# Causal mask of the score maxima: from TensorE products to a VectorE add-and-maximum

## The reference

```python
scores = jnp.einsum('bhqd,bhkd->bhqk', Q, K) / scale
causal = jnp.tril(jnp.ones((s, s), dtype=bool))
scores = jnp.where(causal, scores, jnp.float32(-100000.0))
A = jax.nn.softmax(scores, axis=-1)
```

## Time and profile before

| | |
|---|---|
| median of three runs | 945.94 us (940.37 to 948.93) |
| the profiled execution | 943.07 us, span 941.3 us |
| mean granted TensorE clock | 0.889 of full speed |
| TensorE busy | 694.3 us, 74% |
| VectorE busy | 472.5 us, 50% |
| ScalarE busy | 359.9 us, 38% |
| GpSimd busy | 332.1 us, 35% |

### The profile page before, as it was taken

One profiled execution on the slowest core, in us unless ns is written; L12 is line 12 of the kernel. 1 busy time (PEld: TensorE's weight loads), 2 busy tenths in 40 slices (PEclk: granted clock), 3 DMA queues, 4 the chain that ended last, 5 costly groups with the idle time before them and its releaser, 6 DMA issues.

```text
span 941.3 us, 14542 instructions
## 1 busy us (share of the span) xinstructions
PE 694.3 (74%) x4531; PEld 480.2 (51%) x4531; DVE 472.5 (50%) x1013; ACT 359.9 (38%) x912; POOL 332.1 (35%) x324
## 2 busy tenths in 40 slices
PE   0441222374678888987899888999859999999993
PEld 0441111142233343533345442788749999989983
DVE  6435556597676776485777874445411122111210
ACT  0122333244358654456364557411203222322220
POOL 1113454485688852301141116301612211111222
PEclk9856555596599999999999999899999999999997
DMA  6999788689674302998911003676979999999971
GB/s 214 303 264 304 274 283 306 227 285 331 202 228 155 113 2 101 276 330 267 373 61 46 1 2 122 237 253 218 305 233 303 331 311 327 311 339 378 348 199 22
DMA packets 136207, 216.15 MB, mean 230 GB/s; under 512 B 10357, under 2 KB 102058, under 8 KB 135978
## 3 DMA queue, kind: packets, MB, share of 16 engines
q1 hardware_dynamic: 114808, 150.78, 48.4%
q0 software_dynamic: 16784, 61.51, 21.3%
q10 hardware_dynamic: 4546, 3.08, 1.1%
HBM read 160.87 MB, written 56.37 MB: 231 GB/s over the span
## 4 chain that ended last, share of the span: by engine, by line
DMA 33%; PE 29%; DVE 18%; issue 9%; POOL 6%; ACT 2%; SPq 1%; POOLq 1%; DVEq 0%; ACTq 0%
DMA results<-arena,home 13%; DVE arena L1752 8%; DMA result<-arena,home 7%; PE psum L1455 6%; PE psum L1281 5%; DMA arena<-table,tap_col 4%; PE psum L1469 3%; PE psum L1517 3%; POOL pairs_x L1034 3%; DMA arena<-padded,band_col 3%; DMA arena<-qk_rows 3%; PE psum L1526 2%; PE psum L1415 2%; PE psum L1294 1%; PE psum L1322 1%
## 5 line engine op out<-in xcount | busy, mean ns | idle before, releaser
L1201 ACT ACTIVATE arena<-psum 128x512 f32<-128x512 f32 (+3 forms) x384 | 170.2, 491 | 131.1 <-PE psum L1469 99.0
L1752 DVE TENSOR_REDUCE arena<-psum 128x2 f32<-128x1024 f32 (+2 forms) x192 | 176.0, 954 | 61.6 <-PE psum L1287 47.0
L1251 ACT ACTIVATE arena<-psum,b_cols 128x128 f32<-128x128 f32 x312 | 84.7, 382 | 232.4 <-PE psum L1517 229.1
L1526 PE MATMUL psum<-arena 128*128 128x256 f32 x624 | 144.6, 386 | 11.5 <-DVE arena L2084 11.5
L1517 PE MATMUL psum<-arena 128*128 128x128 f32 x1248 | 148.2, 278 | 6.5 <-issue 3.6
L1517 PEld LDWEIGHTS psum<-arena 128*128 128x128 f32 x1248 | 146.9, 194 | 9.7 <-issue 8.1
L1281 PE MATMUL psum<-arena 96*128 96x512 bf16 (+3 forms) x384 | 107.5, 347 | 34.3 <-DMA arena<-qk_rows 17.8
L1526 PEld LDWEIGHTS psum<-arena 128*128 128x128 f32 x624 | 117.7, 194 | 27.8 <-issue 12.8
L1469 PE MATMUL psum<-arena 99*128 99x512 bf16 (+3 forms) x384 | 110.6, 333 | 15.7 <-ACT arena L1201 10.0
L2080 DVE TENSOR_TENSOR arena<-psum,arena 128x256 f32<-128x256 f32 x39 | 16.5, 424 | 162.1 <-PE psum L1526 78.0
L1281 PEld LDWEIGHTS psum<-arena 96*128 96x128 bf16 x384 | 35.5, 102 | 105.6 <-DVE arena L1752 53.8
(11 more groups left out here) (213 smaller groups left out, 937.8 us busy)
## 6 DMA issues: line engine op xcount, KB each, us to landing
arena<-L_ffn_W SPq DMA_DIRECT2D x78, 1024.0 KB, 7.6
pairs_x<-zeros SPq DMA_DIRECT2D x4, 4160.0 KB, 25.4
arena<-qk_rows SPq DMA_DIRECT2D x16, 768.0 KB, 10.8
table<-arena SPq DMA_DIRECT2D x20, 384.0 KB, 9.4
qk_rows<-arena SPq DMA_DIRECT2D x16, 384.0 KB, 5.8
arena<-pairs_x SPq DMA_DIRECT2D x39, 130.0 KB, 6.6
qk_rows<-arena SPq DMA_DIRECT2D x16, 256.0 KB, 6.0
padded<-arena SPq DMA_DIRECT2D x2, 1328.0 KB
```

The source lines that it names most:

```text
L1201: nc.scalar.activation(probs[at % 2][h][:, q0:512], banks[turn % SCORE_BANKS][:, q0:512], ACT.Exp, scale=DH ** -0.5).then_inc(exp_done, 1)
L1251: ins = nc.scalar.activation(hidden_t[k % SLOTS][:, f], banks[hidden_bank(k) + f // 4][:, (f % 4) * P:(f % 4 + 1) * P], ACT.Relu, bias=b1_ ...
L1526: ins = t_.matmul(banks[5][:, 0:D], hidden_t[u][:, f], w2_slot[u][:, f], start=f == 0, stop=f == FC - 1)
L1752: return v.reduce_max(part[:, 2 * pair:2 * pair + 2, qb], psum[:, first:first + 2, 0:keys], AX_X)
```

## The change

The diagonal chunks get no mask product. `largest` keeps `reduce_max` for a pair of chunks without a diagonal. For a diagonal pair it issues two instructions, one for each head: each adds the mask to the head's chunk in PSUM (in place), and takes the maximum of the sums into one column. The mask operand is a window `mask_wide` of the constants' tile: up to 384 columns of zeros, then the triangle, in f32, cut so that the triangle stands under the last 128 keys. To make the zeros neighbours of the triangle, the zeroed block moves into `cst`, ahead of `mask_qk`; VectorE waits once for it to be cleared. The bf16 copy of `mask_qk` is gone.

```diff
-CONST_PARTS = [("sheared", JB), ("row", SB), ("identity", P), ("mask_qk", P), ("mask_kq", P), ("before", P),
+CONST_PARTS = [("sheared", JB), ("row", SB), ("mask_qk", P), ("identity", P), ("mask_kq", P), ("before", P),
...
+ZERO_W = 2 * ROW
...
-    CONST_AT[_name] = (CONST_W, _width)
+    CONST_AT[_name] = (CONST_W + ZERO_W * (CONST_W >= FIRST_CONST), _width)
...
-        cst = sb("cst", [P, CONST_W])
+        cst = sb("cst", [P, ZERO_W + CONST_W])
+        zeros = cst[:, FIRST_CONST:FIRST_CONST + ZERO_W]
+        mask_wide = cst[:, FIRST_CONST + ZERO_W - 3 * P:FIRST_CONST + ZERO_W + P]
...
-        zeros = sb("zeros", [P, 2 * ROW])
...
-        mask_qk = sb("mask_qk", [P, P], BF16)
...
-            sp.dma_start(cst[:, FIRST_CONST:CONST_W], consts[:, FIRST_CONST:CONST_W]).then_inc(consts_in, 16)
+            sp.dma_start(cst[:, ZERO_W + FIRST_CONST:ZERO_W + CONST_W], consts[:, FIRST_CONST:CONST_W]).then_inc(consts_in, 16)
...
-                diagonal = qb // 4 == kc
...
-                                start=True, stop=not diagonal)
-                if diagonal:
-                    at_ = qb * P - kc * 512
-                    ins = t_.matmul(bank[:, at_:at_ + P], ident_b[:], mask_qk[:], start=False, stop=True)
+                                start=True, stop=True)
...
-            pe.wait_ge(masks_set, 3)
+            pe.wait_ge(masks_set, 2)
...
             dve.wait_ge(consts_in, 16)
+            dve.wait_ge(zeros_set, 1)
...
-            for o, name in ((ident_b, "identity"), (mask_qk, "mask_qk"), (mask_kq, "mask_kq")):
+            for o, name in ((ident_b, "identity"), (mask_kq, "mask_kq")):
...
-                return v.reduce_max(part[:, 2 * pair:2 * pair + 2, qb], psum[:, first:first + 2, 0:keys], AX_X)
+                if qb // 4 != kc:
+                    return v.reduce_max(part[:, 2 * pair:2 * pair + 2, qb], psum[:, first:first + 2, 0:keys], AX_X)
+                for k in range(2):
+                    ins = v.tensor_tensor_reduce(psum[:, first + k, 0:keys], psum[:, first + k, 0:keys],
+                                                 mask_wide[:, 4 * P - keys:4 * P], 1.0, -3.0e38, ALU.add, ALU.max,
+                                                 part[:, 2 * pair + k, qb:qb + 1])
+                return ins
```

More of the change, by code:

```diff
@@ L847, in _ @@
         def _(pool):
-            nc.gpsimd.memset(zeros[:], 0.0).then_inc(zeros_set, 1)
+            nc.gpsimd.memset(zeros, 0.0).then_inc(zeros_set, 1)
             for b in range(NB):
```

## The result

The changed kernel takes 953.5 us (median of 20 runs, 946.81 to 958.8) against 946.25 us for the kernel before on the same chip (20 runs). The ratio is 1.0082, 95% interval 1.0060 to 1.0103: 0.6 to 1.0% slower. The forecast of 956 us, 940 to 972, holds. The profiled execution took 953.8 us (span 952.1) beside 943.07 (span 941.3) of before.

A forecast was written before the change was run, and what follows sets the result against it. VectorE alone was taken to bound the prologue, both engines nearly full later. +4.6 us there, then 12.6 on VectorE less 8.1 of TensorE's relief, plus 1 for lost cover, made +10: 956 us, range 940 to 972.

The forecast's parts named there:

- What bounds the stage: Before the first head group's attention VectorE alone sets the time; later TensorE and VectorE wait for each other, both near full.
- e: Time added on VectorE per diagonal pair by two instructions replacing one reduce: 0.34 us, bounded by 0.06 and 0.66.
- The prologue: Maxima before the first head group's attention: 16 pairs by 0.34 us, less 0.8 for masks, +4.6 us.
- that sign: Forecast is wrong if the stretch 222.8 to 244.5 us lengthens by less than 2 us or more than 8.
- TensorE's relief: Removing 256 mask products gains all 8.1 us that line 1287 has on the chain between 247 and 560 us.
- VectorE's extra work: Diagonal pairs on the path, 16 before the attention and 37 later, cost 0.34 us each: 5.4 and 12.6 us.
- the sum: Whole change, 53e - 8.9 + 1: +10 us, giving 956 us beside the median; break-even at e = 0.15.
- The lost cover: Steps with two diagonal 512-column pairs gain 0.68 us on VectorE against 0.64 idle; ten such steps add 1 us.
- Costed at nothing: In-place PSUM write, dropped mask cast, moved zeros and VectorE's wait for the zeroed block: no cost or gain on the path.

The follow-up runs named there:

- either kind of load put on VectorE: Changed kernel with mask products put back on TensorE: 957.65 us; kernel before with a 96-column reduce added behind each diagonal pair's reduce: 964.96 us.
- the constants alone: Kernel before with only the zeroed block moved into the constants' tile and VectorE's wait for it: 947.07 us, ratio 0.9997.
- masks and add: Changed kernel with the mask products put back on TensorE, so the mask is applied twice: 957.65 us, ratio 1.0121.

## Why the prediction held, step by step

- **What bounds the stage.** Right: the prologue is VectorE's alone. In the steps both engines are near full; either kind of load put on VectorE cost 11.5 to 14 us, and the relief on TensorE gave 4.7.
- **e, the term that was mis-sized.** It was taken at 0.34, from a pace of 0.66 plus 0.07 for the column, a head of 0.74. Measured are 0.65 a head and e = 0.158. The form of the instruction and the nearest row for its pace were right (0.66, 0.65 measured with the column); the column's 0.07 was wrong, since its readout starts together with the next instruction. The Trainium skill ("VectorE: DVE Perf Modes", section "Two Vector instructions with no wait between them") is right that such an operation is two instructions: the trace lists 256 readouts of 0.142 us. Start to start they cost nothing against the scalar-tensor-tensor's 0.66 us and 0.05 against the plain add's 0.60, not 0.142.
- **The prologue.** 16e less 0.8 was 4.6 us at e = 0.34 and is 1.7 at 0.158; measured is 1.6. Formula and masks' share (0.9 measured) stand. The prediction called itself wrong if the prologue stretched by less than 2 us, and by that sign it was, on e.
- **TensorE's relief.** 8.1 us, all that the chain of waits put on line 1287, plus 0.8; measured 4.7 (2.5 to 7.0). This step failed by about half as a total. The profile says where it went: the steps at full clock gave 4.8 us back in groups 1 to 7 and the prologue 0.9, and longer steps behind more falls of the clock, in group 0 too, took part of it away. Why the clock falls more often there stays open.
- **VectorE's extra work.** 53e + 1 was 19 us; measured 11.5 (6.2 to 16.6). With the true e the same formula gives 9.4. In the profile 4.7 us of it lie in steps at full clock and 8.7 in the others.
- **So the sum was right by luck: two errors that cancel.** With e = 0.158 put in, 53e - 8.9 + 1 is +0.5 us: no change would have been forecast, and in the steps at full clock there is none. The e taken too large stands for 9.6 us too much; what stands against it, with no term in the prediction, are the steps with a lowered clock.
- **The lost cover.** Expected were steps of 4.3 to 4.5 us in place of 4.13 and VectorE's idle under 0.2. The inner steps kept their length (4.42, 3.89, 3.98 us in group 1 after, 4.36, 4.01, 3.92 before). With the true e a step with two diagonal pairs of 512 columns has 0.32 us more on VectorE, less than its 0.64 of idle, so the cover holds. The last step ahead of the maxima's transpose grew instead, by 0.57 and 0.63 us in groups 0 and 1 of the first profile and by 0.23 where no clock is missing in it, with TensorE waiting 1.90 us for the last pair instead of 1.43; behind that wait the clock fell in two of three executions, at either group.
- **Costed at nothing.** The bank written in place: confirmed by the rate of a column. The moved constants and the new wait: confirmed by the constants alone (0.9997). The dropped cast has no run of its own.

What stays open: which wait brings a fall. Most falls in the attention stand behind waits of TensorE for VectorE, 0.6 to 2.4 us long in the changed kernel, but the same wait comes with and without one, and the total of the waits doesn't rank the kernels: masks and add wait 57.3 us ahead of the maxima's products with 15.4 us of clock missing, the changed kernel 63.6 with 8.5. Filling two such waits brought no gain that shows.

The one version faster than both is the kernel without the mask in the maxima (0.9950). Subtracting an upper bound in place of a row's maximum leaves a softmax unchanged until its exponentials underflow, so it holds for data like these and is no general replacement.

## What to carry to other kernels

Where two engines are both near full, work moved from one to the other is judged by both prices: here 0.06 us slots taken off TensorE gave 4.7 us and 0.16 us a pair put on VectorE took 11.5. A share of the chain of waits is not yet what its removal gives: 8.1 us stood there behind the prologue, and 4.7 came in all, 0.9 of them in the prologue. Where the clock can fall, add up the steps with and without a fall separately, and profile one program more than once: three executions of the same kernel differ here by 9.7 us. Size each side by a kernel with that side alone before trusting a sum that comes out right.

## What was not expected of the hardware

- The accumulator's readout is listed with 0.142 us and adds 0.05 at most: read start to start, not by duration.
- An add and maximum with one f32 stream out of PSUM and one out of SBUF, its sum written back to PSUM, runs at 1.02 ns a column. The Trainium skill ("Vector Engine (DVE) Microarchitecture Reference", section "Points that are easy to get wrong") halves the rate of the scalar-tensor-tensor layout for two SBUF sources that are not bf16; with one of them in PSUM this instruction shows no such loss.
- TensorE's granted clock falls to 0.50 (1.2 GHz) within a stage in which it is busy 85% of the time, mostly behind waits for VectorE such as the 1.90 us at the transposes, where a fall loses 1.06 us on the path; the number of falls in one program varies from execution to execution (5, 9 and 6).
